# Output projection of attention as three products of bf16 halves in place of one f32 product

## What is computed

```python
out = jnp.einsum('bhqk,bhkd->bqhd', attn, V).reshape(B, S, H * dv)
return out @ Wo + bo
```

## Time and profile before

| | us |
|---|---|
| median of 3 runs | 3774.37 |
| lowest, highest | 3768.81, 3776.14 |
| the profiled execution's own time | 3771.53 |
| its span, first to last instruction | 3769.8 |

### The profile page before, as it was taken

How to read it: one execution, slowest core, us unless ns; L and a number is a source line. 1 busy time by engine, 2 the same in 40 slices (tenths; PEclk the granted TensorE clock), 3 DMA queues, 4 the chain that set the end, 5 groups by cost and what they waited for, 6 DMA issues and landing times. The chain is left out here.

```text
span 3769.8 us, 91854 instructions
## 1 busy us (share of the span) xinstructions
PE 3253.7 (86%) x34982; PEld 2529.3 (67%) x34982; DVE 2706.7 (72%) x6150; ACT 1503.5 (40%) x2989; POOL 1643.3 (44%) x2049
## 2 busy tenths in 40 slices
PE   6999998599999999999966114996699999998986
PEld 6888887488888888887842102775367767765765
DVE  5888886588888888888847786552366666666876
ACT  3444443166666666666643101321233333332221
POOL 2555555266666666666630101677100000005776
PEclk9999999599999999999989556998799999998998
DMA  4666665556565656665636101444333333226775
GB/s 142 193 193 190 189 188 156 141 133 171 141 175 142 168 145 165 152 158 147 162 108 194 30 0 50 129 124 119 96 108 103 108 106 105 96 82 162 196 196 146
DMA packets 450399, 519.29 MB, mean 138 GB/s; under 512 B 63917, under 2 KB 419979, under 8 KB 449572
## 3 DMA queue, kind: packets, MB, share of 16 engines
q1 hardware_dynamic: 428552, 474.63, 44.5%
q0 software_dynamic: 21504, 39.94, 4.0%
HBM read 308.37 MB, written 215.94 MB: 139 GB/s over the span
## 5 line engine op out<-in xcount | busy, mean ns | idle before, releaser
L848 DVE TENSOR_REDUCE p_mx<-p_psS 98x2 f32<-98x390 f32 (+1 forms) x1024 | 526.2, 555 | 0.0
L797 ACT ACTIVATE p_probs<-p_psE 98x392 f32<-98x392 f32 x1024 | 449.1, 495 | 0.0
L794 ACT ACTIVATE p_after<-p_psF 98x392 f32<-98x392 f32 x512 | 254.9, 498 | 472.1 <-PE p_psF L940 463.9
L842 DVE COPY_PREDICATED p_psS<-p_later,p_psD 98x196 f32<-98x196 uint32 x1024 | 330.1, 361 | 110.2 <-PE p_psS L926 101.8
L743 POOL TENSOR_SCALAR_AFFINE_SELECT p_after<-p_after 98x392 f32<-98x392 f32 x512 | 273.7, 535 | 233.8 <-ACT p_after L794 233.5
L1285 POOL COPY sb_wt<-sb_gw 112x8 f32 (+1 forms) x28 | 7.4, 264 | 760.7 <-DMA sb_gw<-scratch_gw 760.6
L747 POOL TENSOR_SCALAR_AFFINE_SELECT p_probs<-p_probs 98x392 f32<-98x392 f32 x512 | 273.8, 535 | 85.5 <-ACT p_probs L797 80.0
L1291 POOL DMA_INDIRECT sb_ye<-scratch_ye,sb_idx x224 | 245.9, 1098 | 83.0 <-issue 59.1
L963 PE MATMUL p_psO<-p_probs,p_v 98*32 98x196 f32 x4096 | 279.4, 345 | 2.3 <-POOL p_probs L747 2.2
L1275 POOL DMA_INDIRECT scratch_xe<-sa_xs,sa_idx x224 | 221.0, 986 | 112.6 <-issue 76.4
L419 POOL TENSOR_TENSOR p_rt<-p_rt 128x784 f32<-128x784 f32 x64 | 187.1, 2923 | 122.7 <-DVE p_st L397 122.7
(11 more groups left out here) (287 smaller groups left out, 10398.6 us busy)
## 6 DMA issues: line engine op xcount, KB each, us to landing
scratch_stack<-p_st SPq DMA_DIRECT2D x64, 784.0 KB, 6.1
p_x<-in_x SPq DMA_DIRECT2D x32, 1176.0 KB, 9.5
p_L<-scratch_stack SPq DMA_DIRECT2D x192, 196.0 KB, 4.3
p_U<-scratch_stack SPq DMA_DIRECT2D x192, 196.0 KB, 4.4
scratch_xe<-p_zero SPq DMA_DIRECT2D x32, 1024.0 KB, 5.8
ex_xin<-scratch_xe SPq DMA_DIRECT2D x64, 512.0 KB, 4.0
scratch_ye<-ex_y SPq DMA_DIRECT2D x64, 512.0 KB, 2.8
scratch_h<-p_h SPq DMA_DIRECT2D x32, 392.0 KB
```

Source lines behind the costliest of these rows:

```text
L794: act.activation(after[c][:].rearrange("p h t -> p (h t)"), psF[:, 0:4 * TILE], ACT.Exp, scale=DK ** -0.5).then_inc(p_ok.sem, 1)
L797: act.activation(probs[c][:, b, :], psE[:, b, 0:PAIR], ACT.Exp, scale=DK ** -0.5).then_inc(p_ok.sem, 1)
L842: nc.vector.copy_predicated(own[:, :, c * TILE:(c + 1) * TILE], later[:].unsqueeze(1).broadcast_to([TILE, 2, TILE]), upper).then_inc(chose ...
L848: nc.vector.tensor_reduce(mx[g1][:, c, 4 * q1 + 2 * b:4 * q1 + 2 * b + 2], own, AX.X, ALU.max).then_inc(s_max.sem, 1)
```

## The change

The weights `wo` are split once into halves `woh` and `wol` by GpSimd, before its first position. ScalarE writes the transposed rows as bf16 `atth` where it wrote f32 `attnT`. VectorE writes the rest, `attl`, in the position of `wo`, after its masked copies and before its reduces. TensorE waits for `attl` and makes six bf16 products, three for each half of the 256 rows of Wo, in place of two f32 ones. The semaphore of `attnT` becomes two, and one is new for the halves of wo.

```diff
@@ -541,6 +541,7 @@
+        woh, wol = sb("woh", [128, 2, C], BF16), sb("wol", [128, 2, C], BF16)
@@ -553,7 +554,7 @@
-        attnT = sb("attnT", [128, 2, TILE])
+        atth, attl = sb("atth", [128, 2, TILE], BF16), sb("attl", [128, 2, TILE], BF16)
@@ -571,6 +572,7 @@
+        made_wo = semaphore(nc, ctx, "p2_wo_halves")
@@ -578,7 +580,8 @@
-        at_ok, att_ok, wo_ok, h1_ok = signal("attnT_in_psum", 2), signal("attnT", 2), signal("wo", 2), signal("h1", 2)
+        at_ok, atth_ok, attl_ok = signal("attnT_in_psum", 2), signal("attnT_hi", 2), signal("attnT_lo", 2)
+        wo_ok, h1_ok = signal("wo", 2), signal("h1", 2)
@@ -779,11 +782,14 @@
+                nc.gpsimd.tensor_copy(woh[:], wo[:]).then_inc(made_wo, 1)
+                pool.wait_ge(made_wo, 1)
+                nc.gpsimd.tensor_tensor(wol[:], wo[:], woh[:], ALU.subtract).then_inc(made_wo, 1)
                 positions(pool, position)
@@ -810,13 +816,13 @@
-                        act.activation(attnT[:], psM[:, 0:2 * TILE].rearrange("p (h t) -> p h t", h=2), ACT.Copy).then_inc(att_ok.sem, 1)
+                        act.activation(atth[:], psM[:, 0:2 * TILE].rearrange("p (h t) -> p h t", h=2), ACT.Copy).then_inc(atth_ok.sem, 1)
@@ -842,6 +848,12 @@
                                                       upper).then_inc(chosen.sem, 1)
+                    what, t = TAIL.get(2 * q + c, (None, 0))
+                    if what == "wo" and known(k, 1, IMAGES + 1):
+                        dve.wait_ge(atth_ok.sem, atth_ok.at(k - 1, t + 1))
+                        nc.vector.tensor_tensor(attl[:], psM[:, 0:2 * TILE].rearrange("p (h t) -> p h t", h=2), atth[:],
+                                                ALU.subtract).then_inc(attl_ok.sem, 1)
+                    if known(s1, 0, SLOTS):
                         for b in range(2):
                             own = psS[:, b, 0:PAIR].rearrange("p (h t) -> p h t", h=2)[:, :, 0:S - 1 + c]
@@ -932,6 +943,7 @@
                     if isinstance(s, int) and s == 0 and c == 0:
                         pe.wait_ge(made_v32, 4)
+                        pe.wait_ge(made_wo, 2)
@@ -1005,10 +1017,8 @@
                         if what == "wo":
-                            pe.wait_ge(att_ok.sem, att_ok.at(k - 1, t + 1))
-                            for j in range(2):
-                                last = nc.tensor.matmul(psM[0:TILE, 0:C], attnT[:, j, :], wo[:, j, :],
-                                                        start=(j == 0), stop=(j == 1))
+                            pe.wait_ge(attl_ok.sem, attl_ok.at(k - 1, t + 1))
+                            last = three_products(nc, psM[0:TILE, 0:C], [(atth[:, j], attl[:, j], woh[:, j], wol[:, j]) for j in range(2)])
                             last.then_inc(wo_ok.sem, 1)
```

More of the change, by code:

```diff
@@ L785, in _ @@
             def _(act):
-                for s in (p_ok, ot_ok, en_ok, att_ok):
+                for s in (p_ok, ot_ok, en_ok, atth_ok):
                     s.open(act)
@@ L818, in _ @@
             def _(dve):
-                for s in (chosen, s_max, mch, mrow_ok, nrm, num_ok, h1_ok):
+                for s in (chosen, s_max, mch, mrow_ok, nrm, num_ok, attl_ok, h1_ok):
                     s.open(dve)
@@ L865, in position @@
                         nc.vector.tensor_tensor(ea[:], cn, mt[:], ALU.add).then_inc(mch.sem, 1)
-                    what, t = TAIL.get(2 * q + c, (None, 0))
                     if what == "mtr" and known(k, -1, IMAGES - 1):
```

## The result

The changed kernel took 3791.06 us (median of 5 runs, 3781.89 to 3794.28) against 3773.80 for the kernel before (5 runs, 3768.81 to 3776.14): a ratio of 1.0044, 95% interval 1.0029 to 1.0059. That is 17.3 us slower, where +9.2 was forecast; 3791.06 lies in the range of 3773 to 3795, above the 3779 to 3789 of the forecast's own case. The profiled execution took 3791.06 us with a span of 3789.3, 19.5 more than the span before.

What follows compares the result with a forecast made beforehand. It took a loop of VectorE's run without slack and TensorE's stream as the bound. Subtraction +16.7, second-tile gains -6.5 (even images) and -1.0 (odd) sum to +9.2: 3783.6 us, range 3773 to 3795.

Steps and rivals of the forecast that it cites:

- the forecast's own case: Attention slows by 9.2 us in all, to a median of 3783.6 us, own range 3779 to 3789; chance 0.60.
- the loop of two parts: An image is VectorE's run from quad 1, half 1 to quad 3, half 0, then TensorE's own stream for the rest.
- VectorE's run: First output projection to row-maxima copy, 7.1 us without slack; the first tile's subtraction adds 0.27 us an image, +16.7 in all.
- The pause in quad 3, half 0: TensorE's 0.16 us wait for VectorE's reduce before the second bank of psS, once an image; forecast to stay 0.16.
- The first tile: Quad 1, half 1: TensorE's 0.21 us saving buys nothing, as it arrives earlier at a wait ending 0.27 later.
- TensorE's gain: Six bf16 products take 0.73 us where two f32 ones took 0.94: 0.21 us a tile, two tiles an image.
- what costs nothing: TensorE's wait for the subtraction (0.45 and 0.37 us to spare), ScalarE's writes, GpSimd's halves of wo and two semaphores: nothing.
- The landing itself moves with L870, that is with the VectorE run.: Row maxima sent by SyncE, awaited by the next image's first matmul, land later or earlier as VectorE's copy of them does.
- That the landing doesn't hold odd images: Rival: lateness of the row maxima is chance, so all second tiles keep 0.21 us: +3.5, 3778 us; chance 0.20.
- The dear end: Rival: subtraction costs 0.33 us, nothing kept ahead of odd images, perhaps even ones too: +14.0 to +20.5, 3788 to 3795; chance 0.10.
- TensorE as the bound throughout: Rival: VectorE's run has slack, so each of 126 tiles keeps 0.21 us: -26.5 us, 3748; chance 0.08.
- weight loads that don't hide: Rival: weight loads of the six products are exposed, a second tile 0.44 us dearer: +44 us, 3818; chance 0.02.

Runs made afterwards that it cites:

- e7: The kernel before, with SyncE's three token loads issued behind the odd image's row-maxima sends and GpSimd's copies of v two quads later: 3761.70 us, ratio 0.9964.
- e1: The changed kernel with its two f32 products back, VectorE's subtraction and TensorE's wait for it kept: 3784.95 us, ratio 1.0031.
- e2: The changed kernel without the subtraction, the rows' low half all zeros, six bf16 products kept: 3785.26 us, ratio 1.0026.
- e13: The kernel before, unchanged, run again for a second profile: 3768.19 us in one run.
- e8: The changed kernel with the three token loads issued behind the odd image's row-maxima sends and GpSimd's copies of v two quads later: 3761.35 us, ratio 0.9965.
- e3: The changed kernel with halves and bf16 products for an image's second tile alone, the first tile in f32 without subtraction: 3791.30 us, ratio 1.0052.
- e12: The changed kernel with the subtraction on GpSimd and ScalarE writing the rows twice, token loads not moved: 3810.11 us, ratio 1.0104.
- e14: Same edit as e3, with the token loads issued behind the odd image's row-maxima sends: 3752.53 us, ratio 0.9937.
- e4: The kernel before with SyncE's 1 MB fill issued one position later, behind the load of h0: 3774.34 us, ratio 1.0004.

## Why the prediction was right, and where it was not

**Right: the loop of two parts.** VectorE's run takes the subtraction: it is 0.23 us longer, where 0.27 was worked out. The reduce does begin 0.27 later; that the chain behind it gets 0.04 shorter was not foreseen. The means of E to M grew by 0.25 and 0.30, more than 0.23, because a few images came late into the run or met the low clock (image 19). The pause in quad 3, half 0 stayed (1242.03 to 1242.23), and one of 0.50 us came in quad 2, half 1 as forecast, though split over both banks and with 0.03 to 0.13 of it there before. The first tile bought nothing.

**Right: TensorE's gain,** 0.24 for 0.21; the even image's M to E fell by 0.22. The products are 0.11 us apart with loads of 0.12 us between them, under the matmul before. So the rule of the Trainium skill (TensorE: Matmul & The Clock Gate, Part 3) that a load overlaps only in another row group does not hold for these six either. The reduce starts 0.27 to 0.28 us into a subtraction of 0.35, as rows 4 had it. The Trainium skill (VectorE: DVE Perf Modes, The DRAIN you can't avoid) has it wait for the empty pipe, but lets an operation that nothing holds start earlier; it is the exception that the rows show.

**Right: what costs nothing.** TensorE waited 1.6 us in all for the subtraction, and the first addition came 0.4 us later, so GpSimd's halves of wo are covered.

**Failed: "The landing itself moves with L870, that is with the VectorE run."** It is held mainly by the token loads ahead of it in SyncE's queue; e7 shows it. In the changed kernel two errors nearly cancel: a slower VectorE run lets an odd image hide part of its delay (e1, M to E -0.29), and a faster TensorE loses the even image's gain in the odd one's wait (e2, +0.35). Of that 0.35, 0.19 is the odd image's copy coming earlier and 0.17 the landing coming later, as the loads do: the last token load is issued at 15.6 to 15.7 where the second tile has bf16 products, at 15.2 to 15.5 where it hasn't. Why is not shown. Together the odd image's M to E grew by 0.05 (0.15 against e13), where the sum had -0.03. The account of the changed kernel's attention by the table's means is 62 x 0.275 = +17.1 from E to M, 31 x -0.22 = -6.8 for even images, 31 x 0.05 = +1.6 for odd ones, +11.8 of 12.4 measured; the prediction had +16.7, -6.5 and -1.0. A sum near the truth was thus no proof of the step: the parts apart gave +10 and +10, not +17 and -6.5.

**Missing: TensorE's clock.** The sum has no term for it. In the profile of the changed kernel it costs 3.0 us in image 19 (16.44 for 13.45, against 1.7 in the kernel before) and 5.9 in routing. Attention grew by 12.4 to 16.6 and the median by 17.3, where +9.2 was forecast: that this lies in the range is partly luck, since the range was wide enough for what the sum left out.

**The rivals.** That the landing doesn't hold odd images (3778) was wrong for this kernel, and e8 shows what it would have been worth: -0.4 on e7, where the rival had +3.5. The dear end (3788 to 3795) has the measured time in it, but not its reason: the run grew by 0.23 and not by 0.33, and even images kept their gain. TensorE as the bound throughout fell with the pause in quad 2, half 1; weight loads that don't hide, with their spacing.

**Open.** Why the clock in the routing pass is 0.90 in some profiles and down to 0.85 in others is not shown, nor whether an edit of attention has a part in it; e3, e12 and e14 are edited and have 0.89 to 0.90. Outside attention the two profiles of the kernel before are the shortest of all (2592.9 and 2593.8 us), and those of twelve edited kernels have 2595.7 to 2601.5; up to 6.7 us of that are routing's clock, the rest, up to 4 us behind the routing pass, is not explained.

## What to carry to other kernels

Where a small transfer gates the next step, follow its queue back to the large loads ahead of it before pricing anything else: its landing may be fixed by them, so that time saved on an engine is handed back as waiting, and a long wait may cost clock besides. Move such loads behind the small transfer first; then a part that cost time may gain it. Here the second tile's half went from 16 us over the kernel before (e3) to 26 under it (e14), 11 of them the move's own (e7); the whole change gains nothing on the move alone (e8). And place each half of a change by the engine that has slack there: here the second tile's halves are free and the first tile's are not.

## What the hardware showed that was not expected

SyncE's issue of a stack load took 0.59 to 0.60 us on average in eight of the sixteen places of a pair in the kernel before. The third of the first batch took 0.72 on average in the changed kernel, 0.82 in e2 and 0.85 in e3, and 0.59 with the second tile in f32 products, as before, in e1 and in e4. In part the long issues only change their place: the kernel before has 0.74 to 0.80 at the sixth to eighth. The sixteen of a pair together take 10.2 us there and in e1 and e4, and 10.6, 10.5 and 10.8 in the changed kernel, e2 and e3. The second pair of even sends landed in 2.0 us instead of 1.8 in the changed kernel and in e2. So a change of products on TensorE shows in another engine's issue times; by which way was not tried.
